# Slot-table groups placed between the last shared chunks, and four shared chunks in both runs' fronts

## The reference

```python
def _L1_ffn_ref(x, Wr, Wg, Wu, Wd, Sg, Su, Sd):
    E, K, F = (16, 2, 128)
    FS = 256
    xf = x.reshape(T, d)
    shared = jax.nn.silu(xf @ Sg) * (xf @ Su) @ Sd
    probs = jax.nn.softmax(xf @ Wr, axis=-1)
    topk_p, topk_i = jax.lax.top_k(probs, K)
    cw = jnp.zeros((T, n_exp), x.dtype).at[jnp.arange(T)[:, None], topk_i].add(topk_p)
    def step(acc, ew):
        wg, wu, wd, c = ew
        y = jax.nn.silu(xf @ wg) * (xf @ wu) @ wd
        return (acc + y * c[:, None], None)
    routed, _ = jax.lax.scan(step, jnp.zeros_like(xf), (Wg, Wu, Wd, cw.T))
    return (routed + shared).reshape(b, s, d)
...
    x = x + _L1_ffn_ref(_layernorm(x, axis=-1), L1_ffn_Wr, ...)      # first run, behind L1_attn_a
    x = x + _L1_attn_b_ref(...)
    x = x + _L1_ffn_ref(_layernorm(x, axis=-1), L1_ffn_Wr, ...)      # second run, behind L1_attn_b
```

## Time and profile before

| | us |
|---|---|
| median of 3 runs | 4840.21 |
| lowest, highest | 4834.57, 4848.72 |
| the profiled execution | 4845.29 |
| its span | 4843.6 |
| busy: PE, DVE, ACT, POOL | 3890.5, 2828.1, 2272.6, 2440.0 |
| first run: fronts, middle, tail (from, to) | 3313.18 to 3401.76, to 3443.72, to 3470.04 |
| second run: fronts, middle, tail (from, to) | 4448.17 to 4520.11, to 4579.26, to 4604.38 |

### The profile page before, as it was taken

The page is one execution under the profiler, slowest core; times in us unless marked ns, Lnnn a source line. Parts: engine busy times, 40 slices in busy tenths (PEclk is TensorE's granted clock), DMA queues, the critical chain, the costliest instruction groups (busy, mean ns, idle before and its releaser), DMA issues.

```text
span 4843.6 us, 49570 instructions
## 1 busy us (share of the span) xinstructions
PE 3890.5 (80%) x15210; PEld 2236.3 (46%) x15210; DVE 2828.1 (58%) x4885; ACT 2272.6 (47%) x4371; POOL 2440.0 (50%) x2147
## 2 busy tenths in 40 slices
PE   6888888758975888799688869996886798888891
PEld 2333333346752555577233336664562333334571
DVE  5999999962126676211489872226536776663422
ACT  5666656531116776211466643334444455455451
POOL 5999999932212233311599954443456221112356
PEclk8999999968987999899799979997897799998896
DMA  4555666522220010221355641113354332210244
GB/s 151 162 158 159 159 163 156 152 92 68 87 81 18 18 35 18 89 85 61 119 157 167 158 129 46 45 43 111 101 158 125 90 54 41 41 28 26 70 145 131
DMA packets 310362, 471.88 MB, mean 97 GB/s; under 512 B 34506, under 2 KB 167350, under 8 KB 310026
## 3 DMA queue, kind: packets, MB, share of 16 engines
q1 hardware_dynamic: 276864, 388.61, 29.2%
q0 software_dynamic: 28992, 75.72, 5.5%
q10 hardware_dynamic: 4224, 4.19, 0.2%
HBM read 374.87 MB, written 97.10 MB: 97 GB/s over the span
## 4 chain that ended last, share of the span: by engine, by line
PE 37%; DVE 7%; ACT 5%; issue 4%; POOL 4%; DMA 2%; SPq 0%; DVEq 0%; POOLq 0%; ACTq 0%
PE s_gate_up L2319 8%; PE s_result_sum L2335 4%; PE s_hidden_sum L1755 3%; PE s_result_sum L1766 3%; PE s_out_sum L3739 3%; PE s_scores L3680 2%; PE s_shared L2996 2%; PE s_scores_T L3723 2%; DVE s_maxima L3364 2%; DVE s_decay L370 1%; POOL s_gathered L1043 1%; PE s_shared L3008 1%; PE s_transposed L2309 1%; POOL s_h L435 1%; PE s_mid_transposed L2328 1%
## 5 line engine op out<-in xcount | busy, mean ns | idle before, releaser
L435 POOL TENSOR_TENSOR s_h<-s_dtu,s_bc 128x1024 f32<-128x1024 f32 x384 | 902.1, 2358 | 52.8 <-PE s_y_sum L477 40.5
L477 PE MATMUL s_y_sum<-s_h,identity 128*128 128x512 f32 x1536 | 777.2, 644 | 127.5 <-POOL s_h L444 117.1
L402 ACT ACTIVATE s_decay<-s_dt,s_A 128x512 f32<-128x512 f32 x768 | 498.4, 682 | 309.6 <-DVE s_h L377 302.7
L477 PEld LDWEIGHTS s_y_sum<-s_h,identity 128*128 128x128 f32 x1536 | 295.9, 203 | 572.0 <-issue 302.4
L3536 ACT ACTIVATE s_weights_T<-s_scores_T 128x1024 f32<-128x1024 f32 (+3 forms) x384 | 292.6, 811 | 265.2 <-PE s_scores_T L3723 263.6
L2319 PE MATMUL s_gate_up<-s_w_gate_up,s_rowsT 128*128 x1168 | 414.0, 487 | 2.1 <-issue 1.8
L3364 DVE TENSOR_REDUCE s_maxima<-s_scores 128x1 f32<-128x512 f32 (+3 forms) x463 | 296.7, 659 | 161.4 <-PE s_scores L3684 85.8
L444 POOL TENSOR_TENSOR s_h<-s_h,s_bc 128x512 f32<-128x512 f32 x288 | 365.8, 1271 | 15.3 <-DVE s_h L370 11.1
L2378 DVE TENSOR_TENSOR s_mid<-s_act,s_gate_up 128x128 f32<-128x128 f32 (+1 forms) x225 | 91.5, 407 | 446.6 <-ACT s_act L2351 446.6
L3584 POOL TENSOR_SCALAR_AFFINE_SELECT s_weights_T<-s_weights_T 128x256 f32<-128x256 f32 x256 | 102.6, 406 | 476.6 <-ACT s_weights_T L3536 473.9
L2297 POOL DMA_INDIRECT s_rows<-rows_by_token,s_rows_at x225 | 228.7, 1016 | 190.3 <-issue 94.8
(11 more groups left out here) (536 smaller groups left out, 7657.3 us busy)
## 6 DMA issues: line engine op xcount, KB each, us to landing
s_bc<-s_bc_rows SPq DMA_DIRECT2D x384, 512.0 KB, 5.1
sorted_results<-s_result SPq DMA_DIRECT2D x158, 128.0 KB, 2.2
s_w_inter<-in_L_ffn_experts_inter SPq DMA_DIRECT2D x16, 1024.0 KB, 5.1
s_w_exp_out<-in_L_ffn_experts_out SPq DMA_DIRECT2D x16, 1024.0 KB, 8.1
s_queries<-parts_of_q SPq DMA_DIRECT2D x96, 128.0 KB, 4.6
s_keys<-parts_of_k SPq DMA_DIRECT2D x96, 128.0 KB, 7.3
results_by_token<-zeros SPq DMA_DIRECT2D x16, 512.0 KB, 5.9
s_pair<-results_by_token SPq DMA_DIRECT2D x16, 512.0 KB, 5.9
```

What stands on the lines that cost most here:

```text
L402: S.e.activation(self.decay[:, (2 * g + d) % 4, :], dt[q // self.passes % 2][:, at, :], ACT.Exp, scale=A[:, at, g % ns:g % ns + 1]).then_i ...
L435: G.e.tensor_tensor(self.h[r][:], dtu[q // self.passes % 2][:, at:at + 2, :], mid(self.bc[r][:, 0, :], 2), ALU.mult).then_inc(*self.fed.up())
L477: made = T.e.matmul(self.y[:, d, :], ident[:], self.h[r][:, d, :], start=False, stop=g % ns == ns - 1)
```

## The change

Two things are changed in `moe1_stage`, in both runs unless said otherwise.

The second run gets the first run's order of the fronts: shared chunks 0 to 3 have their gate and up sums behind fronts 0, 2, 4 and 6, and chunks 0 to 2 their outputs behind fronts 1, 3 and 5. It also keeps 4 chunks of transposed rows instead of 8.

The slot table's groups get places by three tables. On ScalarE (`WEIGHED`) group 0 stands between chunk 7's copies and chunk 6's output copies, group 1 behind these, group 2 between the two output copies of chunk 7, group 3 and the others behind them. On TensorE (`PLACED`) group 0 stands behind chunk 6's outputs, group 1 between the two halves of chunk 7's outputs, group 2 and the others behind them. On VectorE (`TILES_AFTER`) the tiles' experts are computed behind group 7 instead of group 2.

```diff
-    if K.owed == "normed":
-        MULTIPLIED, FINISHED, TURNED = {0: 0, 2: 1, 4: 2, 6: 3}, {1: 0, 3: 1, 5: 2}, 4
-    else:
-        MULTIPLIED, FINISHED, TURNED = {1: 0, 4: 1}, {3: 0, 6: 1}, NC
+    MULTIPLIED, FINISHED, TURNED = {0: 0, 2: 1, 4: 2, 6: 3}, {1: 0, 3: 1, 5: 2}, 4
     INSIDE = len(MULTIPLIED)
+    WEIGHED, PLACED, TILES_AFTER = {(7, 0): 1, (7, 1): 1, (8, 0): 1, (8, 1): 1}, {(7, 1): 1, (8, 0): 1, (8, 1): 1}, 7
...
         for g in range(table.GROUPS):
             table.vector_group(g)
-            if g == table.RING - 1:
+            if g == TILES_AFTER:
                 R.vector_tiles()
...
         groups = iter(range(table.GROUPS))
+
+        def weigh(c, i):
+            for g in itertools.islice(groups, WEIGHED.get((c, i), 0)):
+                table.scalar_group(g)
+
         for c in range(INSIDE, NC):
             gate_and_up(c, 0)
             gate_and_up(c, 1)
+            weigh(c, 0)
             if c - 1 not in FINISHED.values():
                 outs(c - 1, 0)
                 outs(c - 1, 1)
+            weigh(c, 1)
         for i in range(2):
-            table.scalar_group(next(groups))
-        outs(NC - 1, 0)
-        outs(NC - 1, 1)
+            outs(NC - 1, i)
+            weigh(NC, i)
...
+        def place(c, i):
+            for g in itertools.islice(groups, PLACED.get((c, i), 0)):
+                table.tensor_group(g)
...
                 made.then_inc(*out_sum.up())
                 free[b] = out_copied.at(2 * c + i // 2)
+                if c == NC - 1:
+                    place(NC, i // 2)
...
         for c in range(INSIDE, NC):
             gate_and_up(c)
+            place(c, 0)
             if c - 1 not in FINISHED.values():
                 outs(c - 1)
+            place(c, 1)
             if c == INSIDE + 1:
                 R.tensor_rank()
-        for i in range(2):
-            table.tensor_group(next(groups))
         outs(NC - 1)
```

More of the change, by code:

```diff
@@ L2999, in gate_and_up @@
                     free[b] = (gated if j == 0 else up_copied).at(FK * c + f)
+        groups = iter(range(table.GROUPS))
+        def place(c, i):
+            for g in itertools.islice(groups, PLACED.get((c, i), 0)):
+                table.tensor_group(g)
         def outs(c):
@@ L3018, in tensor @@
                 outs(FINISHED[c])
-        groups = iter(range(table.GROUPS))
         for c in range(INSIDE, NC):
             gate_and_up(c)
+            place(c, 0)
             if c - 1 not in FINISHED.values():
                 outs(c - 1)
+            place(c, 1)
             if c == INSIDE + 1:
                 R.tensor_rank()
-        for i in range(2):
-            table.tensor_group(next(groups))
         outs(NC - 1)
```

## The result

The changed kernel takes 4813.2 us (median of 5 runs, 4808.4 to 4816.3) against 4840.2 (4834.6 to 4848.7): ratio 0.9942, 95% interval 0.993 to 0.9954. That is 27.0 us less where 30.3 were forecast. The profiled execution took 4809.0 us, span 4807.3.

A forecast was written before the change was run, and what follows sets the result against it. Bound by TensorE in the middles, ScalarE's interrupted group chain in the tails, and waits and slow clock in the second run's fronts. 7.75 + 22.6 = 30.3 us off the 4840.2 median gives 4810, range 4802 to 4824.

The forecast's parts named there:

- both parts: Reordered slot-table groups in both tails (first run gains 7.75 us); four shared chunks in second run's fronts (second run gains 22.6).
- the sum walks through: First run's tail rebuilt step by step from its own durations; `s_rows_at` ends at 3462.3 instead of 3470.05.
- the model: First run's fronts, taken as pattern for TensorE in the second's: first front with gate and up 15.7 us, fronts 73.1.
- part 1: Tails of both runs: ScalarE's groups begin earlier, without the long interruption; first run gains 7.75 us, bounds 0 and 9.4.
- the comparisons beside the additions: Tail, VectorE beside GpSimd: groups 2 and 3 might each pay 1.08 us, group 3's slack falling from 1.9 to about 0.8.
- the rebuilt tail: First run's tail by part 1: last comparison about 3457.7, last table matmuls 3461.0, tile numbers 3461.75 as last wait, costing 0.7 us.
- The clock rival: Second run's fronts: TensorE's clock falls in three rounds, costing about 14 us, total 4824; chance 10%.
- The tail rival: Both tails: each of four TensorE-ScalarE alternations waits 0.8 us more, so each tail loses 3.2 us, total 4816; chance 8%.
- the slower rival: Second run's fronts: clock stays at 1.2 GHz, fronts 127 us instead of 73, costing 54 us, total 4864; chance 2%.

The follow-up runs named there:

- The two experiments with one part each: Kernel before with only the second run's new fronts: 4832.8 us; changed kernel with the second run's old fronts: 4832.7 us; ratio 0.9972 each.
- The experiment with late additions: Changed kernel, GpSimd adding chunks 6 and 7 only behind VectorE's last slot-table comparison, chunk 7's copies in another buffer: 4819.0 us, ratio 0.9945.
- the one with everything together: Changed kernel plus logits behind the shared work, earlier rank matmuls and tiles, chunk 7's additions alone behind the last comparison: 4796.2 us, ratio 0.9907.
- the run with later logits: Changed kernel with TensorE making a chunk's logits behind the shared work that follows its front, in both runs: 4810.5 us, ratio 0.9926.
- its second measurement: The changed kernel again, without edit, in a later job: 4813.2 us, ratio 0.9948.

## Why the prediction was right, and where it was off

**The mechanism was right in both parts, and they add up.** The tails' interruption is gone, with the queue order that the sum walks through, and the second run's fronts hold the moved chunks for 1.4 us where I had 1.2. Fronts of 73.4 us were forecast as 73.1. The two experiments with one part each show 12.2 and 14.0 us. That the fronts came out so close is in part luck: of the three sets behind the first, one took 8.81 us where each had been put at 7.03, and the first front with its set took 14.8 us where the model had 15.7.

**One term of part 1 was mis-sized: the comparisons beside the additions.** The prediction had the row (2.30 us against 1.22), named the cost, and then priced it for groups 2 and 3 alone, with 1.08 us each and none for the first comparison of a group, and found slack for it. In fact it hit four comparisons in each tail beside the one that had been slow before, 1.07 us each for either kind, and the additions were slowed too, so that they lay beside more of them. ScalarE's last group ends 17.0 us behind the middle instead of 15.9, and the tail lasts 20.0 us instead of 18.5. This cost 1.5 us in each run. The experiment with late additions gives the 13.9 us for the last comparison that I had (14.0), and the one with everything together shows the rebuilt tail itself, 17.9 us. The Trainium skill's rule that I cited, from "SBUF — State Buffer", section "SBUF: two separate sides", that the loser waits for the whole instruction, fits the sizes: 1.07 us more, a little under one addition of 1.26 us. By that page of the Trainium skill the small operations of the tiles, which have one SBUF input, should be held only in VectorE's two-port modes; here they took 0.84 to 1.38 us beside additions instead of 0.20 to 0.40, and no run shows in which mode they ran.

**The clock rival happened in part.** I gave it 10% and 14 us. It cost 1.7 us inside the fronts (the 8.81 us set at 4456.65) and 1.7 us at the start of the middle, where I had taken the first run's 41.96 us without asking whether that stretch is always at full clock. In the first run it was, in the profiles before and after; in the run with later logits it wasn't (43.66 us). A sign of it had stood in the fronts that I took as the model, in the trace before, behind the same transposes and the same wait:

```profile
3362.69 1.96 PE L2986 MATMUL s_logits<-s_w_router,s_xT 128*128 128x16 f32 x16 [0.79 <-ACT s_xT L2876]
3364.50 8.81 PE L2996 MATMUL s_shared<-s_xT,s_w_shared_gate_up 128*128 128x512 f32 x16
```

What the Trainium skill describes in "TensorE: Matmul & The Clock Gate", section "A second HAM failure mode: psum-queue depth-cycling", short idles between groups of matmuls that make the clock go back and forth, agrees in part: the slow sets of the second run follow a front with its 0.79 us wait, and they went when the wait was taken away or output sums were put between. But the wait alone doesn't make a set slow. Two of the four that follow it in the changed kernel's second run took 7.11 us, and the set in the first run's fronts that took 8.81 us before took 7.11 us in the changed kernel (at 3364.14) and 8.81 us in its second measurement (at 3361.28). What decides between them stays open.

**The sum.** 30.3 forecast; less 3.0 for the two tails, less 1.7 for the middle, less 0.3 for the fronts is 25.3, and the stretches show 25.4. The medians say 27.0 in the first measurement and 29.4 in the second, with intervals (0.0012 and 0.002 of the ratio) of 6 and 10 us either way, so the times alone couldn't have told 25 from 30.

**The other rivals.** The tail rival put 3.2 us on each tail (its 4816 is 6.4 above the forecast); measured were 1.5 each, and for another reason: not the alternation of TensorE and ScalarE, whose steps came where they were expected, but VectorE. Nothing of the slower rival was seen.

## What to carry to other kernels

When work of one engine is moved earlier, list what runs beside it on the engine that it contends with, over all its instructions and not only the next two, and add the other engine's slowdown too; here a cost that was seen in one row of the profile came back four more times in each tail. Waits too short to look at (0.79 us, eight times) were worth more than the whole reordering of a tail (9.8 us of fronts against 6.3), once work that was already in the queue was put into them; 1.7 of the 9.8 are the slow set that went with them. Compare two profiles by the stretches that the change touches; the others differed by up to 7 us with no cause in the code.

## What the runs showed of the hardware

- VectorE's two-input comparisons of 0.82 and 1.22 us took 1.89 and 2.29 us beside GpSimd's two-input additions, and the additions 1.85 us on average (5.56 for three) or 2.27 instead of 1.26. Even 128x80 casts of 0.20 us on VectorE took 1.18 to 1.22 us there (in three experiments).
- TensorE's clock fell to 0.70 and 0.69 in the first 2.85 and 2.96 us of two sets (of the two levels, 1.2 and 2.4 GHz, the lower one for part of that time) without any wait longer than 0.8 us ahead of it, behind eight transposes, the wait and 16 matmuls of 16 columns. Two more sets behind the same sequence in the same run took 7.11 us, so the sequence alone doesn't bring the fall. With the logits moved behind the shared work and no wait ahead of them, the sets inside the second run's fronts took 7.03 us, the first one apart, in three profiles.
